# Weights times values of a 16-head attention: one 32-column tile a head, one PSUM bank, one eviction and four transposes a unit

## The reference

```python
x = layernorm(x + attn(x, x, x, sa_..., causal=True), ln1_g, ln1_b)
x = layernorm(x + attn(x, ctx, ctx, ca_..., causal=False), ln2_g, ln2_b)
x = layernorm(x + moe(x, router_w, router_b, e_w1, e_b1, e_w2, e_b2), ln3_g, ln3_b)
```

```python
a = softmax(scores, axis=-1)                          # batch, head, query, key
o = einsum('bhqk,bkhd->bqhd', a, V).reshape(Bq, Sq, Dm)
return o @ wo + bo
```

## Time and profile before

| what | us |
|---|---|
| median of 3 runs | 516.17 |
| lowest and highest run | 516.06, 517.64 |
| span of the profiled execution | 518.9 |
| time of the profiled execution beside its span | not given apart from it |
| PE, DVE, ACT, POOL busy in the span | 382.3, 300.0, 283.9, 182.1 |
| start of the attention loop to its last pair | about 19 to 378 |
| experts and last norm | about 378 to 519 |

### The profile page before, as it was taken

The page is one execution under the profiler, slowest core; times in us unless marked ns, Lnnn a source line. Parts: engine busy times, 40 slices in busy tenths (PEclk is TensorE's granted clock), DMA queues, the critical chain, the costliest instruction groups (busy, mean ns, idle before and its releaser), DMA issues.

```text
span 518.9 us, 9401 instructions
## 1 busy us (share of the span) xinstructions
PE 382.3 (74%) x2138; PEld 253.3 (49%) x2139; DVE 300.0 (58%) x1020; ACT 283.9 (55%) x653; POOL 182.1 (35%) x254
## 2 busy tenths in 40 slices
PE   2358688989889889989989888566139889998300
PEld 1324445555545545545545534432129778788300
DVE  9633555677776786786787775363613323333192
ACT  2027169678579678687687686253215444444122
POOL 9303212232432442442432524213113333334354
PEclk9969799999999999999999999758559999999755
DMA  8120320421331432422322320316236555555242
GB/s 239 57 65 0 69 46 23 140 61 25 113 95 30 128 72 44 128 61 56 120 55 68 118 43 14 117 26 201 70 90 171 145 155 158 147 151 166 64 111 81
DMA packets 52595, 48.29 MB, mean 93 GB/s; under 512 B 5322, under 2 KB 45247, under 8 KB 52552
## 3 DMA queue, kind: packets, MB, share of 16 engines
q1 hardware_dynamic: 50248, 43.56, 31.5%
q0 software_dynamic: 2304, 4.24, 2.5%
HBM read 22.12 MB, written 14.85 MB: 71 GB/s over the span
## 4 chain that ended last, share of the span: by engine, by line
PE 36%; DVE 18%; SPq 10%; issue 10%; POOL 9%; DMA 7%; ACT 5%; POOLq 0%; DVEq 0%; ACTq 0%
PE bank L624 5%; PE bank L543 5%; POOL dispatched L1072 4%; PE bank L635 4%; PE bank L487 4%; SPq L372 4%; PE bank L530 3%; PE bank L488 3%; DVE ca_nm L814 2%; PE bank L511 2%; DMA sa_km<-sa_ku 2%; DMA xs<-dispatched 2%; ACT ca_qm L681 2%; PE bank L510 2%; ACT sa_qm L681 2%
## 5 line engine op out<-in xcount | busy, mean ns | idle before, releaser
L740 ACT ACTIVATE sa_us<-bank,expert_b 128x128 f32<-128x128 f32 x160 | 45.9, 368 | 65.2 <-PE bank L624 59.7
L1080 POOL DMA_INDIRECT results<-ca_pt,xs x40 | 39.3, 983 | 70.4 <-DVE ca_pt L991 64.1
L1047 POOL TENSOR_SCALAR_AFFINE_SELECT sa_pt<-sa_pt 128x512 f32<-128x512 f32 x64 | 39.0, 637 | 70.4 <-ACT sa_pt L689 70.0
L814 DVE TENSOR_REDUCE sa_nm<-bank 128x4 f32<-128x512 f32 x64 | 41.5, 684 | 14.3 <-PE bank L511 14.1
L1072 POOL DMA_INDIRECT dispatched<-r_sent,r_row x32 | 32.3, 1008 | 43.8 <-DVE r_sent L940 36.5
L989 DVE TENSOR_TENSOR yb<-bank,late_rows 128x128 f32<-128x128 f32 x40 | 11.7, 292 | 61.8 <-issue 36.5
L635 PE MATMUL bank<-sa_pt,sa_us 128*128 x320 | 46.0, 288 | 0.0
L624 PE MATMUL bank<-xsT,ca_pt 128*128 128x128 f32 x320 | 45.9, 288 | 0.0
L681 ACT CAST sa_qm<-bank 8x512 fp32r<-8x512 f32 x64 | 36.8, 576 | 14.1 <-PE bank L518 12.4
L681 ACT CAST ca_qm<-bank 8x512 fp32r<-8x512 f32 x64 | 36.8, 575 | 9.6 <-PE bank L518 8.4
L624 PEld LDWEIGHTS bank<-xsT,ca_pt 128*128 128x128 f32 x320 | 40.7, 199 | 1.9 <-issue 0.8
(11 more groups left out here) (209 smaller groups left out, 856.6 us busy)
## 6 DMA issues: line engine op xcount, KB each, us to landing
ca_pt<-in_e_w SPq DMA_DIRECT2D x40, 256.0 KB
dispatched<-filler SPq DMA_DIRECT2D x17, 520.0 KB, 4.4
sa_km<-sa_ku SPq DMA_DIRECT2D x32, 96.0 KB
sa_qm<-sa_qu SPq DMA_DIRECT2D x32, 96.0 KB
ca_qm<-ca_qu SPq DMA_DIRECT2D x32, 96.0 KB
xs<-dispatched SPq DMA_DIRECT2D x40, 65.0 KB
sa_pt<-in_e_w SPq DMA_DIRECT2D x8, 256.0 KB, 4.6
ca_pt<-results SPq DMA_DIRECT2D x8, 256.0 KB, 5.3
```

The costliest lines, as they stand in the source:

```text
L740: act.activation(hid[b][:, c, :], bank[2 * b + c // 2][:, P * (c % 2):P * (c % 2) + P], ACT.Gelu, bias=b1[:, bass.ds(expert * FC + c, 1)]) ...
L814: dve.tensor_reduce(k.nm[:, u, g, :], bank[home[k, "scores", u][g % 2]][:, :].rearrange("q (j n) -> q j n", j=J)[:, :, 0:k.keys], AX.X, AL ...
L1047: pool.affine_select(out=blockg, in_=blockg, compare_op=ALU.is_ge, fill=0.0, base=0, pattern=[[0, J], [1, P]], channel_multiplier=-1).then ...
L1080: pool.indirect_dma_start(out=results, out_offset=bass.IndirectOffsetOnAxis(ap=xs[v][:, P:P + 1].bitcast(I32), axis=0), in_=ys[v], in_offs ...
```

## The change

Each head gets its own 32 columns of vo: 8 values, one column of ones, 23 zeros. mix multiplies head j of group g, vo[:, u, 4g + j, :], with that head's 128 columns of pt, on the array's columns 32j to 32j + 31, and writes partitions 32j to 32j + 31, columns 128g to 128g + 127 of a bank. So a unit has 16 matmuls of 128 columns in place of 4 of 512, and all 16 heads lie in the first bank of home[k, "mix", u]. That bank is taken at the first half and given back after the second. ACT copies it once a unit, at the place of the second half. restore has one part, at the place of the second half; it transposes four blocks into the second bank of the table, and DVE does one reciprocal over 16 sums and one multiplication over 128 values. The four entries restore 0 and restore 2 of SA and CA leave ORDER. us has half its size, vo twice; the setup clears vo with two operations a kind in place of one.

```diff
-            k.vo = t("vo", [keys, 2, GROUPS, 64])
+            k.vo = t("vo", [keys, 2, HEADS, 32])
-            k.us = [t(f"us{u}", [P, 2, 512]) for u in range(2)]
-            k.rd = t("rd", [P, 2, 2, 2, J])
+            k.us = [t(f"us{u}", [P, 512]) for u in range(2)]
+            k.rd = t("rd", [P, 2, HEADS])
...
-        SETUP = 15
+        SETUP = 17
...
-            (CA, "scores", 0, -1), (RT, "choose", 0, -2), (SA, "restore", 0, 0), (SA, "mix", 1, 0),
+            (CA, "scores", 0, -1), (RT, "choose", 0, -2), (SA, "mix", 1, 0),
...
             def mix(k, p, part):            # PE
                 u, half = divmod(part, 2)
                 if part == 0:
                     pe.wait_ge(k.s_vo, p + 1)
+                b = home[k, "mix", u][0]
+                if half == 0:
+                    take(b)
                 for g in (2 * half, 2 * half + 1):
-                    b = home[k, "mix", u][g // 2]
                     pe.wait_ge(k.s_pm if k.causal else k.s_ex, p * 8 + 4 * u + g + 1)
-                    if g % 2 == 0:
-                        take(b)
-                    ins = pe.matmul(bank[b][64 * (g % 2):64 * (g % 2) + 64, :], k.vo[:, u, g, :], k.pt[u][:, 512 * g:512 * g + 512], start=True, stop=True)
-                    if g % 2:
-                        ins.then_inc(k.s_u_ps, 1)
-                        give(b, k.s_us, p * 4 + 2 * u + g // 2 + 1)
+                    for j in range(J):
+                        ins = pe.matmul(bank[b][32 * j:32 * j + 32, P * g:P * g + P], k.vo[:, u, J * g + j, :],
+                                        k.pt[u][:, 512 * g + P * j:512 * g + P * j + P], start=True, stop=True)
+                ins.then_inc(k.s_u_ps, 1)
+                if half:
+                    give(b, k.s_us, p * 2 + u + 1)
 
             def restore(k, p, part):        # PE
-                u, h = divmod(part, 2)
-                b = home[k, "mix", u][h]
+                u = part // 2
+                b = home[k, "mix", u][1]
                 take(b)
-                pe.wait_ge(k.s_us, p * 4 + 2 * u + h + 1)
-                for j in range(J):
-                    ins = pe.transpose(bank[b][:, P * j:P * j + P], k.us[u][:, h, P * j:P * j + P], ident)
+                pe.wait_ge(k.s_us, p * 2 + u + 1)
+                for g in range(GROUPS):
+                    ins = pe.transpose(bank[b][:, P * g:P * g + P], k.us[u][:, P * g:P * g + P], ident)
...
             def mix(k, p, part):            # ACT
-                u, h = divmod(part, 2)
-                act.wait_ge(k.s_u_ps, p * 4 + 2 * u + h + 1)
+                u, half = divmod(part, 2)
+                if half == 0:
+                    return
+                act.wait_ge(k.s_u_ps, p * 4 + 2 * u + 2)
...
-                act.copy(k.us[u][:, h, :], bank[home[k, "mix", u][h]][:, :]).then_inc(k.s_us, 1)
+                act.copy(k.us[u][:, :], bank[home[k, "mix", u][0]][:, :]).then_inc(k.s_us, 1)
...
-                setup(dve.memset(k.vo[:, :, :, 32:64], 1.0))
+                setup(dve.memset(k.vo[:, :, :, HD:HD + 1], 1.0))
+                setup(dve.memset(k.vo[:, :, :, HD + 1:], 0.0))
...
             def restore(k, p, part):        # DVE
...
+                heads = bank[home[k, "mix", u][1]][:, :].rearrange("q (h r) -> q h r", h=HEADS)
+                dve.reciprocal(k.rd[:, u, :], heads[:, :, HD]).then_inc(k.s_rd, 1)
+                dve.wait_ge(k.s_rd, p * 2 + u + 1)
+                dve.tensor_tensor(k.on[:, u, :].rearrange("q (h d) -> q h d", h=HEADS), heads[:, :, 0:HD],
+                                  k.rd[:, u, :].rearrange("q (h o) -> q h o", o=1).to_broadcast([P, HEADS, HD]), ALU.mult).then_inc(k.s_on, 1)
```

36 lines of the change are left out of this document (14 added, 22 removed).

## The result

The changed kernel takes 533.05 us (median of 4 runs, 530.36 to 534.83) where the kernel before took 516.90 beside it (4 runs, 516.06 to 519.80): a ratio of 1.028 with a 95% interval of 1.023 to 1.033. It is slower by 16 us where 12.5 us less were forecast.

The account below looks back on a forecast made before the run. PE was taken as close to full, the chain of waits as deciding; savings of 2.8 (ramp), 6.0 (loop), 1.4, 0.3 and 2.0 (tail) sum to 12.5 off the 516.2 us median: 503.7 us, range 497 to 510.

Parts of the forecast that it names:

- What a half costs: Half a unit of the values product: 0.60 us after the change, 0.41 less than the 1.01 on the chain before.
- the lower bound from the earlier trace: Half a unit of the product: 16 weight-load and matmul pairs at 0.03 us, 0.48, about equal to the array's time.
- Rivals 1 and 2: Product halves: instruction hand-out keeps them near 1.0, 507.5 us, 17%; or narrow tiles do not overlap, 1.86, 526 us, 8%.
- The other parts: Each unit loses four transposes (0.44 us), one ACT copy (0.587) and a DVE reciprocal and multiply pair (0.31 saved).
- the longer clearing: Setup on DVE: clearing vo takes +1.1 us, hidden because the casts that follow end only with POOL's operations.
- 1.00 in the loop: Attention loop: PE's granted clock stays at 1.00 (2.4 GHz) after the change, as in the profile before.
- rival 3: Attention loop: with less work PE's granted clock falls and the gain is lost; 522 us at 0.80; chance 5%.
- The rival's break-even: Attention loop: the 1.2 us saved are lost once 11% of PE's chain time is slow, clock about 0.94.
- Its price at 0.80: Attention loop at clock 0.80: +16 us over five iterations, 522 us in all.
- the -6.0 of the loop: Five full iterations between 88 and 276 us: 1.2 us saved in each, together -6.0.
- the -1.2 an iteration: One loop iteration: two restores save 0.31 each, two SA halves 0.15 together, the SA restore after them 0.44.
- It costs nothing in the loop: CA norm of unit 0 waits about 0.6 us for the single eviction, covered by POOL's scatter; 0.7 in the last pair.

Follow-up runs that it names:

- e11: Kernel before with only self-attention changed, plus dummy matmuls ahead of the waits of the shift and first scores; ratio 0.990.
- e13: Changed kernel without the indirect scatter (memsets instead), plus dummy matmuls ahead of the waits of the shift and first scores; 509.7 us, one run.
- e16: Second run of e11's kernel (only self-attention changed, dummy matmuls ahead of waits), beside a dummies-only control on the same chip; ratio 0.994.
- e6: Changed kernel with the four indirect scatters an iteration replaced by one-column memsets; 516.0 us, one run.
- e10: Changed kernel with the four indirect scatters an iteration replaced by plain transfers of the same rows to fixed places; 513.9 us, one run.
- e7: Kernel before with the four indirect scatters an iteration replaced by one-column memsets; 510.5 us, one run.
- e1: Changed kernel plus a full-array dummy matmul of 256 columns ahead of each half of the product; ratio 1.029.
- e4: Kernel before with only the product changed to four 32-column tiles; each half keeps its own bank and eviction; ratio 1.026.
- e3: Changed kernel with the two banks of cross-attention's unit 1 exchanged, so its first norm no longer waits for the single eviction; ratio 1.018.
- e5: Kernel before with only self-attention changed; cross-attention keeps its 64-column tiles, two evictions and four restores a pair; ratio 0.999.
- e14: Kernel before with its 64-column product cut into eight 128-column matmuls a half, and without the indirect scatter; 527.7 us, one run.
- e9: Kernel before with its 64-column product cut into matmuls of 128 columns, eight a half in place of two; ratio 1.041.

## Why the prediction was wrong

**What a half costs: right.** 0.60 us was forecast, 0.57 is measured. Four tiles do overlap: 16 records in 0.46 us and a drain, as the lower bound from the earlier trace rows had it. Rivals 1 and 2, which had 25% together, are out. The prediction also had an estimate of 0.99 from the Trainium skill ("TensorE: Matmul & The Clock Gate", section "Wait — 56ns, not 53.3ns?"), which gives about 62 ns of the sequencer per matmul without hardware decoding. It counted 16 records; a half has 8 matmul instructions, for which that figure gives an estimate of 0.50. The trace has the 16 records start within 0.37 us, so 0.99 is out, and the figure itself isn't tested.

**The other parts: nearly right in size.** Half of the copies went (16 of 0.59 us are left for each kind), half of the transposes too. DVE's reciprocal and multiply take 0.57 us together (262.23 to 262.80 in one iteration), where 0.45 was forecast, so a unit saves 0.19 there and not 0.31. The start did not move: the second `sa_ku` addition of the first pair starts at 22.7 against 23.1, so the longer clearing was hidden as argued.

**"1.00 in the loop": the first step that failed.** The sum took every duration at full clock, and rival 3 had 5%, because "the gaps left in an iteration stay under 1 us or so, while those of the later stretch are over 2". That argument compared single gaps with a stretch that was a different kind of work. The trace of before showed the clock held at 33.9 us busy of 37.6; nothing in it showed it held with less to do. After the change an iteration with 31.0 busy of 38.2 has 0.91, and with dummies ahead of waits 1.00 comes back in all five iterations of e11's profile and in some of e13's and e16's. The rival's break-even, a clock of about 0.94, was usable: without the scatter, iterations at 0.95 take 37.6 against 37.3 of the control. Its price at 0.80 wasn't: +16 over the five iterations and -6.5 outside them make 525.7, not 522. The term that failed is the -6.0 of the loop. Without the scatter the five iterations of the changed kernel take 190.4 us in e6 and 186.8 in e10, against 186.4 in the control e7: 4.0 and 0.4 us more. Even at full clock the -1.2 an iteration was twice too large; 0.6 is what the four iterations there keep.

**"It costs nothing in the loop": the second step that failed.** The new wait of the CA norm behind the single eviction was seen, its cover named (POOL's scatter until 214.34), and its size, 0.6, taken from the copy alone. The order of events was right. What the step lacked is the lateness of the increment in front of the copy: 0.5 to 2.5 us, up to 3.0 in e1 and e4, where many short matmuls run beside the indirect scatter. The norm waits 1.2, 1.7, 2.2, 2.3 and 2.7 us beside the five scatters of the loop, and in the later ones POOL has ended its scatter by then, so the cover is gone. But the wait isn't the cause either: with the norm freed (e3, 1.018) or the eviction split (e4, 1.026) most of the loss stays, since the increments behind are late too. No rival had this. The product was then 2 matmuls a half and its increments came within 0.03 us; but the late increment of the transposes, 0.5 us behind the scatter, stood in the trace of before already.

**The sum as measured.** On the chip of e6 and e7 the changed kernel would take 518.2 x 1.028 = 532.7 us. Without the scatter it is 516.0, 16.7 less; the kernel before loses 7.7 (518.2 to 510.5). The difference, 9 us, is the lateness and what hangs on it; 5.5 is what is left of clock and gain. Both terms rest on single runs on a chip where runs of the kernel before spread from 511.6 to 524.1, so each is good to a few us. The first is borne out by the iterations, in which the changed kernel loses 6.3 us more to the scatter in four of them. The second isn't: 3.0 of the 5.5 us are e6's first iteration, 40.1 at a clock of 0.87, which took 36.9 in e10 and 36.3 in e13.

**What stays open.** The two conditions are shown, each taken away by itself: short matmuls in number (e5, and the kernel before) and the indirect form of the transfer (e6, e10, e14). Why they hurt each other isn't. Only TensorE's increments are late: between 120 and 300 us of the changed kernel all of ScalarE's and VectorE's that the trace has come within 0.02 us of the recorded end. The product's late ones there come 0.6 to 1.1 us after one of GpSimd's four instructions has ended, all but the first, and whether the matmuls themselves or only their increments are held, no record tells, as their ends are modelled. It is open too why the scatter itself costs the kernel before 0.4 us an iteration; its one late increment isn't on the chain, as VectorE is then still waiting for `ca_rs` (until 215.34). And how much of the clock's fall comes from the waits is open: the changed kernel's iterations have 0.87 to 0.91 with the scatter and, in e6, 0.91 to 0.95 without it.

## What to carry to other kernels

Work taken out of TensorE in a loop that is just busy enough for the full clock is not a gain until the clock after it is known; give every duration at both levels. Filling waits with dummy matmuls raised the clock here, but bought no time that the runs can show. Cutting one matmul into many cost nothing on TensorE's own timeline with four narrow tiles (with two wide ones it cost 0.5 us a half, e9), yet it can make its increments late beside an indirect transfer; change only the part that doesn't lie beside one. An edit in two symmetric halves is worth trying one half at a time: here one half carried the whole loss and the other the small gain.

## What was not expected of the hardware

- Beside GpSimd's indirect scatter (four instructions of about 1 us), the increments of TensorE's product came up to 3.0 us after the recorded ends, with 8 short matmuls a half; with 2 long ones 0.03, without the scatter or with plain transfers of the same rows under 0.06. In the kernel before, that of eight transposes in a row was 0.5 to 0.6 us late.
- PE's granted clock was 1.00 in an iteration with 33.9 us busy of 37.6, 0.91 in one with 31.0 of 38.2 and 0.87 in one with 32.2 of 40.6; with SA alone changed, 1.7 us of dummies an iteration ahead of waits brought it from 0.95 to 1.00 in one profiled execution and to 0.95 to 1.00 in another.
- A dummy matmul ahead of every half (0.43 us each) left the time of the changed kernel unchanged: 1.029 against 1.028.
- The records of four 32-column tiles start about 7 ns apart, each four 0.09 to 0.11 us behind the last; a half of 16 records takes 0.57 us on the chain.
